# Mixture-of-experts routing: normalised rows stored in order, 32 byte records scattered, rows gathered by indirect transfers

## What is computed

```python
logits = xf @ Wr + br
topk_w, topk_idx = jax.lax.top_k(logits, TOP_K)
topk_w = jax.nn.softmax(topk_w, axis=-1)
gate = jnp.sum(jax.nn.one_hot(topk_idx, NUM_EXPERTS, dtype=xf.dtype) * topk_w[..., None], axis=1)
h = jax.nn.relu(jnp.einsum('th,ehf->etf', xf, W1) + b1[:, None, :])
y = jnp.einsum('etf,efh->eth', h, W2) + b2[:, None, :]
out = jnp.einsum('te,eth->th', gate, y)
```

## Time and profile before

| what | value |
|---|---|
| median of three runs | 2469.1 us |
| the profiled execution | 2486.94 us |
| its span, first to last instruction | 2485.2 us |
| PE busy | 2104.7 us (85%) |
| VectorE busy | 1781.9 us (72%) |
| GpSimd busy | 892.3 us (36%) |
| expert stage, first to last tile | about 2021 to 2422 us |
| L1284 accumulate | 104 times, 1552 ns each |
| L904 scatter | 96 times, 964 ns each |

### The profile page before, as it was taken

The page is one execution under the profiler, slowest core; times in us unless marked ns, Lnnn a source line. Parts: engine busy times, 40 slices in busy tenths (PEclk is TensorE's granted clock), DMA queues, the critical chain, the costliest instruction groups (busy, mean ns, idle before and its releaser), DMA issues. The chain is left out here.

```text
span 2485.2 us, 59391 instructions
## 1 busy us (share of the span) xinstructions
PE 2104.7 (85%) x21124; PEld 1268.0 (51%) x21125; DVE 1781.9 (72%) x3303; ACT 1074.4 (43%) x2468; POOL 892.3 (36%) x781
## 2 busy tenths in 40 slices
PE   0447999999999999998999998984998739999990
PEld 0432444444444444444444444432877639999980
DVE  8429999999999999998999998992344424444440
ACT  2014555555555565555555565551111114444430
POOL 1043244344344444443443442411133334444441
PEclk6567999999999999999999999987999769999995
DMA  4122333333333333333333333325666258898878
GB/s 148 36 70 53 91 86 97 98 88 94 97 91 90 104 92 88 102 94 87 101 93 90 84 91 89 92 70 179 222 229 224 88 149 210 211 214 212 211 170 205
DMA packets 207992, 306.99 MB, mean 124 GB/s; under 512 B 59552, under 2 KB 151200, under 8 KB 207648
## 3 DMA queue, kind: packets, MB, share of 16 engines
q1 hardware_dynamic: 173216, 252.26, 36.2%
q0 software_dynamic: 21888, 39.20, 8.1%
q10 hardware_dynamic: 12672, 12.58, 1.5%
HBM read 154.07 MB, written 80.64 MB: 94 GB/s over the span
## 5 line engine op out<-in xcount | busy, mean ns | idle before, releaser
L629 ACT ACTIVATE a_prob<-ps_s,a_nmax 128x768 f32<-128x768 f32 x768 | 686.3, 898 | 626.7 <-DVE a_nmax L748 626.7
L748 DVE TENSOR_REDUCE a_nmax<-ps_s 128x1 f32<-128x768 f32 x768 | 698.3, 948 | 102.0 <-PE ps_s L561 91.3
L754 DVE STREAM_TRANSPOSE a_probT<-a_prob 128x768 f32<-128x768 f32 x768 | 698.9, 951 | 16.8 <-ACT a_prob L629 16.8
L561 PE MATMUL ps_s<-a_kT,a_qT 64*128 64x384 f32 x3072 | 638.1, 531 | 85.3 <-ACT a_prob L629 72.9
L568 PE MATMUL ps_o<-a_probT,a_vrep 32*64 32x384 f32 x12288 | 565.2, 494 | 29.3 <-DVE a_probT L754 29.1
L561 PEld LDWEIGHTS ps_s<-a_kT,a_qT 64*128 64x128 f32 x3072 | 266.5, 192 | 434.3 <-ACT a_prob L629 294.5
L690 POOL TENSOR_TENSOR a_o<-a_o,a_invrow 128x1536 f32<-128x1536 f32 x32 | 110.5, 3452 | 880.0 <-DMA a_invrow<-inv_d 864.6
L568 PEld LDWEIGHTS ps_o<-a_probT,a_vrep 32*64 32x64 f32 x12288 | 245.5, 132 | 322.2 <-issue 133.3
L448 POOL TENSOR_TENSOR a_prod<-a_raw,a_table 128x384 f32<-128x384 f32 x312 | 303.5, 1007 | 59.4 <-ACT a_raw L621 55.8
L1284 POOL DMA_INDIRECT acc_d<-e_y,e_row_i x104 | 161.5, 1552 | 250.2 <-DVE e_y L1304 246.8
L915 PE MATMUL ps_ra<-wo,r_oT 128*128 128x256 f32 x768 | 192.1, 407 | 40.3 <-DMA r_oT<-oT_d 24.4
(11 more groups left out here) (203 smaller groups left out, 1335.4 us busy)
## 6 DMA issues: line engine op xcount, KB each, us to landing
e_w<-in_L_ffn_W_dram SPq DMA_DIRECT2D x104, 512.0 KB
a_qT<-a_qp SPq DMA_DIRECT2D x512, 96.0 KB, 2.2
a_vrep<-a_vraw SPq DMA_DIRECT2D x512, 48.0 KB, 1.9
a_invrow<-inv_d SPq DMA_DIRECT2D x64, 384.0 KB, 5.1
oT_d<-a_o SPq DMA_DIRECT2D x32, 768.0 KB, 3.5
r_oT<-oT_d SPq DMA_DIRECT2D x64, 384.0 KB, 6.4
e_x<-xs_d SPq DMA_DIRECT2D x104, 132.0 KB
acc_d<-v_zero POOLq DMA_DIRECT2D x8, 768.0 KB, 10.8
```

What stands on the lines that cost most here:

```text
L561: last = pe.matmul(S[:, s % 2, r, 0:HALF], qT[rows, par, 2 * hp + c, P * t:P * t + P], kT[rows, par, :], start=True, stop=True)
L629: act.activation(prob[:, s % RING, :].rearrange("p (r k) -> p r k", r=2), S[:, s % 2, :, 0:HALF], ACT.Exp, bias=nmax[:, s % RING:s % RING ...
L748: v.tensor_reduce(nmax[:, s % RING:s % RING + 1], S[:, s % 2, :, 0:HALF], AX.XY, ALU.max, negate=True).then_inc(max_ready, 1)
L754: v.transpose(turned(par, s), prob[:, s % RING, :]).then_inc(t_ready, 1)
```

## The change

The wide table `xs_d` is gone. There are two: `xn_d`, the normalised rows in token order plus one block of zero rows, and `meta_d`, records of 8 floats (32 bytes: token number, two experts, two gates, padding) by slot. `place` writes the records into buffers of their own, `meta`, and GpSimd's 12 indirect DMAs a batch scatter these. ScalarE stores the 768 rows of a batch with one direct DMA (`store_xn`) and frees the buffer after waiting for it to land. SyncE writes the zero rows at the start of `route`, before it loads anything of `r_oT`, after waiting for GpSimd's constants; the pad rows are now pad records.

In `experts` SyncE loads the records of each tile, eight tiles ahead, the first four before anything else. VectorE copies the token numbers of tile j+4 into a ring (`source`), and GpSimd gathers the rows of tile j+4 with an indirect DMA (`fetch`), ahead of its wait for y of tile j. `gates` reads the record from `meta[:, j]`, a tile-wide table of all 104 tiles, instead of from the ring of x.

```diff
-DX = D + 8
+MX = 8
...
                 oT_b = oT_d.rearrange("(b g) p h s -> b p g h s", g=KV)
                 sp.dma_start(wo[:], io["Wo"].rearrange("(k p) n -> p k n", p=P)).then_inc(wo_in, 16)
                 sp.nop().then_inc(oT_free, 3)
+                sp.wait_ge(const, 9)
+                sp.dma_start(xn_d[TOK:TOK + P, :], blank[:]).then_inc(pads_stored, 16)
...
                 for x in range(NE):
                     row = sp.value_load(tail_i[0:1, x:x + 1], min_val=x * STRIDE, max_val=x * STRIDE + TOK)
-                    sp.dma_start(xs_d[bass.ds(row, P), :], pads[:]).then_inc(zeroed, 16)
+                    sp.dma_start(meta_d[bass.ds(row, P), :], pads[:]).then_inc(zeroed, 16)
                 sp.wait_ge(zeroed, 16 * NE)
                 sp.wait_ge(h_stored, 16 * NB)
+                sp.wait_ge(pads_stored, 16)
+                for q in range(2):
+                    sp.wait_ge(xn_stored[q], 16 * (NB // 2))
                 for q in range(2):
                     sp.wait_ge(scattered[q], NB // 2 * TT * TOPK * 16)
...
                 with pool.Fori(0, NB // 2) as k:
                     for q in range(2):
                         hold(pool, idx_ready, k * 2 + q + 2)
                         for t in range(TT):
                             for e in range(TOPK):
-                                pool.indirect_dma_start(out=xs_d, out_offset=bass.IndirectOffsetOnAxis(ap=idx[:, q, e, t:t + 1], axis=0),
-                                                        in_=xn[:, q, t, :], in_offset=None).then_inc(scattered[q], 16)
+                                pool.indirect_dma_start(out=meta_d, out_offset=bass.IndirectOffsetOnAxis(ap=idx[:, q, e, t:t + 1], axis=0),
+                                                        in_=meta[:, q, t, :], in_offset=None).then_inc(scattered[q], 16)
                         pool.wait_ge(scattered[q], k * (TT * TOPK * 16) + TT * TOPK * 16)
-                        pool.nop().then_inc(xn_free, 1)
+                        pool.nop().then_inc(meta_free, 1)
...
-                def exp_gap(b):
+                def store_xn(b, q):
+                    hold(act, xn_ready, b + 1)
+                    act.dma_start(xn_d[bass.ds(b * SEQ, SEQ), :].rearrange("(t p) d -> p t d", p=P), xn[:, q]).then_inc(xn_stored[q], 16)
+
+                def exp_gap(b, q):
                     act.wait_ge(gap_ready, b + 1)
                     act.activation(ex[:], dl[:], ACT.Exp).then_inc(ex_ready, 1)
+                    act.wait_ge(xn_stored[q], (b >> 1) * 16 + 16)
+                    act.nop().then_inc(xn_free, 1)
...
                 def iteration(b, q):
                     if not first(b):
+                        store_xn(b - 1, 1 - q)
                         turned(b - 1)
                         if not isinstance(b, int):
                             load(b + 1, 1 - q)
-                        exp_gap(b - 1)
+                        exp_gap(b - 1, 1 - q)
                     root(b)
                     store(b)
...
-                    v.tensor_copy(xn[:, q, :, D].bitcast(I32), tok_i[:, b, :])
-                    v.tensor_copy(xn[:, q, :, D + 1:D + 1 + TOPK], top[:])
-                    v.tensor_copy(xn[:, q, :, D + 3], gr[:])
-                    v.tensor_tensor(xn[:, q, :, D + 4], ex[:], gr[:], ALU.mult)
+                    v.wait_ge(meta_free, b + 1)
+                    v.tensor_copy(meta[:, q, :, 0].bitcast(I32), tok_i[:, b, :])
+                    v.tensor_copy(meta[:, q, :, 1:1 + TOPK], top[:])
+                    v.tensor_copy(meta[:, q, :, 3], gr[:])
+                    v.tensor_tensor(meta[:, q, :, 4], ex[:], gr[:], ALU.mult)
...
-        x, xT = sb("e_x", [P, RING, DX]), sb("e_xT", [P, 2, D])
+        x, xT = sb("e_x", [P, RING, D]), sb("e_xT", [P, 2, D])
+        meta, from_i = sb("e_meta", [P, NT, MX]), sb("e_from_i", [P, RING], U32)
...
-        def loop(eng, tile):
+        def loop(eng, tile, last=1):
 
             for n in range(RING):
                 tile(n, n)
-            with eng.Fori(1, NT // RING - 1) as k:
+            with eng.Fori(1, NT // RING - last) as k:
                 for n in range(RING):
                     tile(k * RING + n, n)
-            for n in range(RING):
-                tile(NT - RING + n, n)
+            for j in range(NT - last * RING, NT):
+                tile(j, j % RING)
...
                 def load(j, n):
                     row = sp.value_load(at(src_i, j), min_val=0, max_val=SLOTS - P)
-                    sp.dma_start(x[:, n, :], xs_d[bass.ds(row, P), :]).then_inc(x_in[n], 16)
+                    sp.dma_start(meta[:, bass.ds(j, 1), :].rearrange("p o m -> p (o m)"), meta_d[bass.ds(row, P), :]).then_inc(meta_in[n], 16)
...
                 for n in range(RING):
                     load(n, n)
+                for n in range(RING):
                     load_w1(n, n)
+                    hold(sp, meta_in[n], 16)
+                    load(RING + n, n)
 
                 def tile(j, n):
+                    if more(j, 2 * RING):
+                        hold(sp, meta_in[n], (j >> 2) * 16 + 32)
+                        load(j + 2 * RING, n)
                     if more(j, RING):
-                        hold(sp, xt_done, j + 1)
-                        hold(sp, gate_ready, j + 1)
-                        load(j + RING, n)
                         hold(sp, h_done, j + 1)
                         load_w1(j + RING, n)
 
-                loop(sp, tile)
+                loop(sp, tile, 2)
...
             @block.gpsimd
             def _(pool):
+                def fetch(j, n):
+                    hold(pool, from_ready, j + 1)
+                    pool.indirect_dma_start(out=x[:, n, :], out_offset=None, in_=xn_d,
+                                            in_offset=bass.IndirectOffsetOnAxis(ap=from_i[:, n:n + 1], axis=0)).then_inc(x_in[n], 16)
+
                 def tile(j, n):
+                    if more(j, RING):
+                        hold(pool, xt_done, j + 1)
+                        fetch(j + RING, n)
                     hold(pool, y_ready, j + 1)
                     q = n % 2
                     if not (isinstance(j, int) and j < 2):
@@ -1284,6 +1314,8 @@
                     pool.indirect_dma_start(out=(acc_d, acc2_d)[q], out_offset=bass.IndirectOffsetOnAxis(ap=row_i[:, n:n + 1], axis=0),
                                             in_=y[:, n, :], in_offset=None, compute_op=ALU.add).then_inc(added[q], 16)
 
+                for n in range(RING):
+                    fetch(n, n)
                 loop(pool, tile)
...
+                def source(j, n):
+
+                    hold(v, meta_in[n], (j >> 2) * 16 + 16)
+                    if not (isinstance(j, int) and j < RING):
+                        hold(v, x_in[n], ((j - RING) >> 2) * 16 + 16)
+                    v.tensor_copy(from_i[:, n:n + 1], meta[:, bass.ds(j, 1), 0:1].rearrange("p o m -> p (o m)").bitcast(U32)).then_inc(from_ready, 1)
+
                 def gates(j, n):
 
-                    hold(v, x_in[n], (j >> 2) * 16 + 16)
                     if not (isinstance(j, int) and j < RING):
                         hold(v, added[n % 2], ((j - RING) >> 1) * 16 + 16)
-                    v.tensor_copy(row_i[:, n:n + 1], x[:, n, D:D + 1].bitcast(U32))
-                    v.tensor_tensor(is_it[:, n, :], x[:, n, D + 1:D + 1 + TOPK], held_by[:, bass.ds(j, 1)].to_broadcast([P, TOPK]), ALU.is_equal).then_inc(gate_dve, 1)
+                    v.tensor_copy(row_i[:, n:n + 1], meta[:, bass.ds(j, 1), 0:1].rearrange("p o m -> p (o m)").bitcast(U32))
+                    v.tensor_tensor(is_it[:, n, :], meta[:, bass.ds(j, 1), 1:1 + TOPK].rearrange("p o m -> p (o m)"), held_by[:, bass.ds(j, 1)].to_broadcast([P, TOPK]), ALU.is_equal).then_inc(gate_dve, 1)
                     hold(v, gate_dve, j * 2 + 1)
-                    v.tensor_tensor(share[:, n, :], is_it[:, n, :], x[:, n, D + 3:D + 3 + TOPK], ALU.mult).then_inc(gate_dve, 1)
+                    v.tensor_tensor(share[:, n, :], is_it[:, n, :], meta[:, bass.ds(j, 1), 3:3 + TOPK].rearrange("p o m -> p (o m)"), ALU.mult).then_inc(gate_dve, 1)
                     hold(v, gate_dve, j * 2 + 2)
                     v.tensor_tensor(gate[:, n:n + 1], share[:, n, 0:1], share[:, n, 1:2], ALU.add).then_inc(gate_ready, 1)
 
                 def tile(j, n):
                     bias_h(j, n)
                     gates(j, n)
+                    if more(j, RING):
+                        source(j + RING, n)
                     if not (isinstance(j, int) and j == 0):
                         bias_y(j - 1, (n - 1) % RING)
 
+                for n in range(RING):
+                    source(n, n)
```

More of the change, by code:

```diff
@@ L804, in route @@
         ve, sd, y, y2, rstd = (sb(f"r_s{n}", [P, TT]) for n in range(5))
-        xn = sb("r_xn", [P, 2, TT, DX])
+        xn, meta = sb("r_xn", [P, 2, TT, D]), sb("r_meta", [P, 2, TT, MX])
         xT = sb("r_xT", [P, KC, SEQ])
@@ L814, in route @@
         gr = sb("r_gr", [P, TT])
```

(18 more changed lines are left out.)

16 lines of the change are left out of this document (8 added, 8 removed).

## The result

After the change the median is 2513.3 us (2512.16 to 2514.01, 4 runs) against 2468.0 us (2465.5 to 2469.69, 4 runs): ratio 1.0184, 95% interval 1.0166 to 1.0202. The kernel is 45 us slower. The forecast was 2497 (range 2472 to 2534).

The account below looks back on a forecast made before the run. The expert stage was taken as bound by PE, with DMA close behind. VectorE's added work 26, expert start 1.7 and blank rows 0.4 made +28 us, 2497 us on the median; range 2472 to 2534.

Parts of the forecast that it names:

- Where the time goes: Nearly all the loss falls in the expert loop: +26 us over 96 tiles, of +28 us in total.
- VectorE's sum: Expert loop: VectorE's own work per tile grows from 3.45 to 4.00 us, more than PE's 3.73.
- the slack of 0.28: Expert tiles: VectorE's spare time per tile before the change, taken as 0.28 us between bounds 0.24 and 0.62.
- 0.20 a hold: VectorE in the expert tiles: each hold was priced at 0.20 us, two of them in `source`.
- The landing of x: Expert tiles: gathered x arrives about 0.15 us late per tile, hidden at a 4.00 us round, cost 0.
- rival C: Expert tiles: x comes late and sets the round once landing exceeds 2.74 us; +69 to +121 us, 2538 to 2590; chance 0.19.
- A: Expert tiles: VectorE becomes the bound; forecast 2497 us, from 2480 to 2533; chance 0.60.
- V: Expert tiles: the experiments' name for A, VectorE's own work per tile, about 4.0 us, sets the round.
- X: Expert tiles: the experiments' name for rival C, gathered x landing late sets the round.
- The start of the experts: Four record loads before the first W1 load delay the first big matmul by 1.7 us (0 to 3.4).
- Routing: Routing stage: no gain from fewer scattered bytes, blank rows cost +0.4 us; wrong if it moves over 2 us.
- rival D: Routing stage: halved scatter bytes give back up to 36 us, total 2461 us; chance 0.06.

Follow-up runs that it names:

- g1_full_steps_on_before: Kernel before the change, with two met holds with newly computed values and a copy at a computed address added to VectorE per loop tile: 2484.8 us, ratio 1.0043.
- g3_cheap_one_tile_early: Changed kernel with `source` behind `bias_y(j-1)`, without its second hold in the loop, and `source` and gather one tile earlier: 2482.7 us, ratio 1.0053.
- g4_and_w1_first: g3_cheap_one_tile_early with two of the four first record loads put behind the first W1 load: 2483.1 us, ratio 1.0037 to the kernel before.
- e2_gather_early: Changed kernel with `source` (still on VectorE) and the gather two tiles earlier: 2504.6 us, ratio 1.0135.
- e1_pool_copy: Changed kernel with the token numbers copied by GpSimd, so VectorE has no `source`: 2506.4 us, ratio 1.0146.
- e3_copy_and_early: Changed kernel with token numbers copied by GpSimd and the gather issued two tiles earlier: 2474.9 us, ratio 1.0017.
- g2_cheap_source: Changed kernel with `source` moved behind `bias_y(j-1)` and its second hold removed in the loop, gather left in place: 2506.4 us, ratio 1.0143.
- e5_plain_x: Changed kernel without the gather; SyncE loads fixed contiguous blocks of `xn_d` (wrong rows), VectorE's work unchanged: 2504.3 us, ratio 1.0132.
- e6_steps_on_before: Kernel before the change, with two met holds and a copy added to VectorE per tile, values and address already in registers: ratio 1.000.
- e7_numbers_by_dma: Changed kernel without `source`; SyncE loads each record a second time for the gather's row numbers, gather left in place: 2609.0 us, ratio 1.0517.
- e8_numbers_early: e7_numbers_by_dma with the gather two tiles earlier: 2607.7 us, ratio 1.0516 to the kernel before.

## Why the prediction was right, and where it was not

**Where the time goes** (right). Among the experts, in the round: 32.7 of the 36.4 us that this stage grew.

**VectorE's sum** (right). Own round 3.45 forecast, 3.44 by `g1_full_steps_on_before`. There was luck in this: the slack of 0.28 was a choice between 0.24 and 0.62, made for ScalarE's waits for `b1_now`, which turned out to be no such evidence (below). The dose gives 3.73 - 3.44 = 0.29. `source` 0.53 forecast, 0.54 in the timeline. Sum 4.00 forecast, 3.98 and 4.01 in the two kernels in which nothing else limits. The price of "0.20 a hold" was too coarse, though: a hold costs that only if its value has to be computed. Two with values at hand took 0.17 us together with the dispatch of the copy behind them.

**The landing of x** (the step that failed). It was costed at 0.15 us per tile, hidden at a round of 4.00, and the wait for x was put into rival C with a chance of 0.19. The chain is the one that was written down, two rounds long. In the changed kernel:

```profile
2200.77 0.20 PEld L1239 LDWEIGHTS ps_ex<-ident,e_x 128*128 128x128 f32 x2 [0.82 <-DMA e_x<-xn_d,e_from_i]
...
2204.87 0.98 POOL L1303 DMA_INDIRECT e_x<-xn_d,e_from_i  x1 [0.30 <-issue]
...
2208.91 0.20 PEld L1239 LDWEIGHTS ps_ex<-ident,e_x 128*128 128x128 f32 x2 [0.81 <-DMA e_x<-xn_d,e_from_i]
```

From a transpose to the gather's start 4.10 us (forecast 5.27 - 0.96 = 4.31), and from there to the transpose that wanted it 4.04, where the forecast had 0.96 of issue and some 2.3 of landing, 3.26. 4.10 + 4.04 = 8.14, halved 4.07: the measured round. So the term of the sum that was too small is the landing, by 0.8 us. Counted as rival C counts it, from the end of the issue, it took 3.06 us: over the 2.74 at which C was to decide, under the 3.5 to 4.5 at which C was priced. C's mechanism was there, at a lower price. Over 75 gathers of the stage the last packet ends 3.53 us after the issue's start in the median (2.83 to 4.30), worked out from the packets. The transfer is short, its beginning is late: the first packet runs 2.9 us after the issue's start. The DMA of three stretches behind the gather of 2204.87 shows what fills that time:

```profile
q1 hardware_dynamic: 199, 0.41, 96.9%
```

```profile
q0 software_dynamic: 77, 0.08, 81.6%
q1 hardware_dynamic: 55, 0.08, 35.6%
```

```profile
q0 software_dynamic: 115, 0.18, 52.0%
q1 hardware_dynamic: 159, 0.03, 25.8%
```

In the first (2205.8 to 2207.0) SyncE's queue q1, with W1, has the 16 engines to 97% and GpSimd's q0 moves nothing; q0 follows in 2207.0 to 2207.6, and in 2207.6 to 2208.9. The sentence from the Trainium skill ("DMA: Bandwidth & Descriptors", "Queues, rings and completion order") that engines take turns between queues gave the hope that the gather need not stand behind W1's backlog. These rows don't show q0 getting turns in that stretch. Whether its packets had been ready and were kept waiting, or became ready only then, they don't tell. But the first gather of the stage shows that it is W1 beside it that costs the time. In `g3_cheap_one_tile_early` it is issued before any W1 load, at 2012.41; its first packet runs 1.69 us later and its last ends at 2.42. In `g4_and_w1_first`, the same kernel but for the order of the first record and W1 loads, W1 is issued at 2019.04 and the gather at 2019.45; the first packet runs after 2.53 us and the last ends at 3.47. The DMA of the 2.5 us behind each issue (packets, MB, share), first `g3_cheap_one_tile_early`, in which all of this gather is done, then `g4_and_w1_first`, in which W1's 0.48 MB runs and nothing of q0:

```profile
q0 software_dynamic: 48, 0.13, 17.6%
q1 hardware_dynamic: 288, 0.01, 6.1%
```

```profile
q1 hardware_dynamic: 234, 0.48, 61.9%
```

No accumulate is on q0 yet at that point, so the growth of 1.05 us is not its doing. What it adds in the loop, where one is issued ahead of each gather, no run separates. An estimate from the fit in the same page's section "Anatomy of one DMA — SWDGE (gpsimd) path", 2.3 us for this size, is near what the first gather shows without W1 (last packet at 2.42, PE starts on it at 2.84) and lower than the 3.53 measured beside W1.

**Two limits at one height.** The prediction treated A and C as alternatives. They hold together: V alone 3.98 to 4.01, X alone 4.03 to 4.04, both 4.075. A likely reason for the last step is that a jitter in either now hits a round with no slack; no run tests it. Either limit alone would have brought the time into the stated range (2504.6 us in `e2_gather_early`, 2506.4 in `e1_pool_copy`), so the time by itself does not confirm A. Nor do most of the signs that were named: the round came to 4.075, but PE is busy for 0.96 and not 0.93, VectorE keeps its wait for `ps_ey`, and ScalarE waits for `b1_now` in 25 tiles. The sign for telling the two apart, PE waiting for x "instead", misled, and so did ScalarE's wait for `b1_now`. It is 156.0 us in 80 tiles of `e3_copy_and_early`, whose round is 3.734 as before the change: it comes with a VectorE that is near its limit (it waits for PE in only 9 tiles there), but does not show that VectorE sets the round.

**The start of the experts** (right in kind). From the first load to the first big matmul 6.5 us before and 8.9 after, +2.4 for +1.7 forecast. The prediction looked at the first gather and found it not last; the big matmul also waits for the transpose of the second tile's x. By the packets that x ends at 2016.58 in the changed kernel and the first W1 at 2016.26, and in `g4_and_w1_first` at 2023.50 against 2022.33: x, not W1, is last.

```profile
2008.66 3.73 SPq L1209 DMA_DIRECT2D e_meta<-meta_d  x4
...
2011.53 0.99 POOL L1303 DMA_INDIRECT e_x<-xn_d,e_from_i  x1 [13.15 <-DVE e_from_i L1343]
...
2017.55 1.27 PE L1249 MATMUL ps_eh<-e_xT,e_w 128*128 128x128 f32 x5
```

**Routing** (open). It was forecast unchanged, and wrong if it moved by more than 2 us. Its length, from the load of Wo to the first expert load, is 297.5, 300.2, 300.7 and 303.5 us in four profiles with the wide table (300.5 in the mean) and 292.7 to 304.5 in ten with records (296.5 in the mean). The spread inside either kind is larger than the 4.0 between the means, so the forecast of no change can't be judged, and rival D is neither shown nor shut out for a few microseconds; `e3_copy_and_early` and the kernel before tie, so no larger gain is there. GpSimd's 96 issues cost the same, 0.96 us each, whatever the bytes.

**The rest.** 36.4 of the 45.3 us lie in the expert stage. In `e1_pool_copy`, `e2_gather_early`, `e3_copy_and_early`, `g2_cheap_source` and `g3_cheap_one_tile_early` 96 times the growth of the round and 3 us of start come within 3 us of the medians' difference (`e2_gather_early`: 26.8 + 3 for 32.7); in `e5_plain_x` 6 us are missing, in the two with a third number load on SyncE 5 to 10. For the changed kernel 9 us are left over that no stage of its profile shows. Against the second profile of before, 2474.86 us, its profiled execution is 37.3 us longer, which the expert stage explains. So the 9 us are not in the profile of this kernel; what they are stays open. The kernel before has medians of 2471.9, 2479.9 and 2472.6 us in the three later sets of runs, against 2468.0 in the first, so a part of them may be no more than this scatter. Of the 16 us by which the forecast was low, 96 x 0.075 = 7 are the round, 0.7 the start, and the rest is in these 9.

## What to carry to other kernels

Before giving a short job to an engine whose busy share is low, add up its own round from the timeline: instructions, holds with computed values, loads of numbers, addresses. Here 42% busy was 3.44 of 3.73 us, and SyncE, which shows no busy time at all, took a third issue with a fixed address but not one with its own number load. When two limits lie close together, remove each alone and both at once: here either alone took 0.03 to 0.10 us off a round that had grown by 0.34, both took off all of it. Where a contiguous load becomes a gather that travels beside large loads, ask for it a tile earlier than the ring suggests: here that took the round from 4.03 to 3.80, with the same instructions on VectorE.

## What the runs showed that was not expected

- A wait that is met and whose value lies in a register costs the sequencer about 0.07 us; one whose value is computed from the loop's counter 0.14 to 0.20 (from the starts of the sequencer's records; 0.17 against 0.42 for the same pair and a copy, `e6_steps_on_before` and `g1_full_steps_on_before`).
- An indirect transfer of 128 rows costs GpSimd 0.96 to 0.98 us to issue, for 32 bytes a row as for 1 KB, scattered or gathered; with accumulate 1.58.
- The first packet of a gather runs 2.9 us after its issue began in the changed kernel, and 2.1 in `e3_copy_and_early`, where it stands at another place relative to the W1 loads (medians over 75 and 82 gathers, from the packets). With no W1 under way it is 1.65 to 1.72: the first gather of eight kernels, and the first three of `e7_numbers_by_dma` and `e8_numbers_early`, whose last packets end 2.38 to 2.55 us after the issue's start.
